# Linear attention on one NeuronCore: reciprocals spread and applied behind the fourth tile's V product, denominators ahead of the values product

## What is computed

```
x = x + attention(layernorm(x))      # linear attention, 16 heads of 32
x = x + ffn(layernorm(x))            # top-2 mixture of 8 experts

attention:  q = elu(xn Wq + bq) + 1, k = elu(xn Wk + bk) + 1, v = xn Wv + bv
            for each t:  kv += k_t v_t^T;  ksum += k_t
                         out_t = (q_t kv) / (q_t . ksum + 1e-6)
            result = out Wo + bo
```

## Time and profile before

| | us |
|---|---|
| median of 3 executions | 1915.71 (1914.94 to 1915.79) |
| the profiled execution, its own time | 1916.06 |
| its span in the profile | 1914.3 |
| TensorE busy | 1890.7 (99%) |
| VectorE busy | 1569.2 (82%) |
| GpSimd busy | 889.8 (46%) |
| ScalarE busy | 663.8 (35%) |
| granted TensorE clock | 0.998 of full speed |

### The profile page before, as it was taken

How to read it: one execution, slowest core, us unless ns; L and a number is a source line. 1 busy time by engine, 2 the same in 40 slices (tenths; PEclk the granted TensorE clock), 3 DMA queues, 4 the chain that set the end, 5 groups by cost and what they waited for, 6 DMA issues and landing times.

```text
span 1914.3 us, 60181 instructions
## 1 busy us (share of the span) xinstructions
PE 1890.7 (99%) x25412; PEld 1659.6 (87%) x25412; DVE 1569.2 (82%) x3356; ACT 663.8 (35%) x1298; POOL 889.8 (46%) x981
## 2 busy tenths in 40 slices
PE   7999999999999999999999999999999999999997
PEld 6888888888888888888888888888888888888887
DVE  7888787888879888778878888887888897888888
ACT  4333333323333332333333433333333333323331
POOL 4345554455443554534554445544345553455422
PEclk9999999999999999999999999999999999999999
DMA  6343234333243432343323334333443234333222
GB/s 215 101 128 112 96 106 128 118 118 112 90 127 119 127 121 74 123 125 116 123 89 118 117 112 136 100 98 113 128 128 112 85 114 130 117 117 113 89 73 90
DMA packets 171197, 217.97 MB, mean 114 GB/s; under 512 B 24368, under 2 KB 85808, under 8 KB 170928
## 3 DMA queue, kind: packets, MB, share of 16 engines
q1 hardware_dynamic: 170928, 214.13, 35.4%
HBM read 151.02 MB, written 63.04 MB: 112 GB/s over the span
## 4 chain that ended last, share of the span: by engine, by line
PE 95%; DVE 2%; POOL 1%; DMA 1%; issue 0%; SPq 0%; ACT 0%; POOLq 0%; DVEq 0%
PE ring L684 38%; PE ring L666 36%; PE ring L758 7%; PE num_ps L788 6%; PE num_ps L771 3%; PE num_ps L801 2%; PE ring L730 1%; PE ring L743 1%; DMA v_tok<-in_wv_t 1%; DVE s_mask L973 0%; PE ring L654 0%; DVE stats L1091 0%; DVE den L1220 0%; DVE res L1084 0%; DVE o_lo L1215 0%
## 5 line engine op out<-in xcount | busy, mean ns | idle before, releaser
L1315 POOL TENSOR_TENSOR k_sum<-k_sum,q_raw 128x512 f32<-128x512 f32 x128 | 165.3, 1291 | 545.0 <-DVE q_raw L984 545.0
L883 ACT ACTIVATE e_tmp<-ring,bias_n 128x512 f32<-128x512 f32 x256 | 175.9, 687 | 509.3 <-PE ring L666 508.7
L973 DVE TENSOR_TENSOR s_mask<-ring,causal 128x512 f32<-128x512 f32 x512 | 315.0, 677 | 0.0
L684 PE MATMUL ring<-wv_hi,xt_hi 128*128 128x260 f32 x1024 | 298.9, 292 | 0.0
L684 PE MATMUL ring<-wv_hi,xt_lo 128*128 128x260 f32 x1024 | 289.2, 282 | 0.0
L684 PE MATMUL ring<-wv_lo,xt_hi 128*128 128x260 f32 x1024 | 289.2, 282 | 0.0
L684 PE MATMUL ring<-wo_hi,o_hi 128*128 128x260 f32 x1016 | 284.8, 281 | 1.3 <-ACT o_hi L938 1.3
L684 PE MATMUL ring<-wo_lo,o_hi 128*128 128x260 f32 x1016 | 285.7, 282 | 0.0
L684 PE MATMUL ring<-wo_hi,o_lo 128*128 128x260 f32 x1016 | 285.5, 284 | 0.2 <-DVE o_lo L1215 0.2
L938 ACT ACTIVATE o_hi<-num_ps 128x512 fp32r<-128x512 f32 x127 | 75.8, 597 | 465.9 <-PE num_ps L788 465.9
L666 PE MATMUL ring<-xt_hi,wk_hi 128*128 128x512 f32 x512 | 207.2, 405 | 3.4 <-DVE xt_lo L1042 1.7
(11 more groups left out here) (147 smaller groups left out, 3955.4 us busy)
## 6 DMA issues: line engine op xcount, KB each, us to landing
x_tok<-in_x SPq DMA_DIRECT2D x128, 256.0 KB, 3.8
res<-in_x SPq DMA_DIRECT2D x128, 256.0 KB, 2.8
out<-res SPq DMA_DIRECT2D x128, 256.0 KB, 2.1
x_in<-in_x_t SPq DMA_DIRECT2D x124, 256.0 KB, 4.7
keys_turned<-k_turned SPq DMA_DIRECT2D x112, 256.0 KB, 2.0
k_tok<-keys_turned SPq DMA_DIRECT2D x448, 64.0 KB, 2.1
x_rows<-moments_rows SPq DMA_DIRECT2D x31, 512.0 KB, 3.6
k_t<-in_wk_t SPq DMA_DIRECT2D x4, 256.0 KB, 4.5
```

Source lines behind the costliest of these rows:

```text
L684: mm = pe.matmul(bank[:, 0:HW], rows[a](k), w[b][:, k, h, :], start=n == 0, stop=n == 3 * KD - 1)
L883: act.activation(e_tmp[:, m], bank, ACT.Relu, bias=bias_n[:, m, g:g + 1], scale=-1.0).then_inc(phi_relu.handle, 1)
L973: dve.tensor_tensor(s_mask[:, j], ring[:, st.bank(u)].rearrange("p (g t) -> p g t", g=KD), repeat(causal, KD), ALU.mult).then_inc(free[st. ...
L1315: pool.tensor_tensor(k_sum[:, g], k_sum[:, g], q_raw[:, g], ALU.mult).then_inc(prod.handle, 1)
```

## The change

- TensorE: in steps with attention, `spread_reciprocals` moves from behind O2 to behind V2, in front of `from_state` of tile 3. `denominators` moves from behind `from_tile` of tile 2 to between `add_state` and `from_tile`. The scores of tile 0 wait for R0 and R1 to be freed, and for a new semaphore `divided` (the first tile's columns of groups 2 and 3); the scores of tile 1 wait for R2 and R3 to be freed.
- ScalarE: the copy of the denominators goes ahead of that of `o_hi`.
- VectorE: `divide` is done behind V2's halves and no more ahead of the moments. It is cut in six: groups 0 and 1 whole, the first 128 columns of groups 2 and 3, then the other 384 columns of groups 2 and 3.
- The ring: R0 to R3 stand behind V2 in the list, and the three skipped uses all stand at the end of the step. So the banks of most uses change; K0's bank (0) was that of V3's first half and is that of its second.

```
-SKIPS = {0: 1, 3: 2}
+SKIPS = {3: 3}
...
         uses += chunk_uses(c, 0, 1)
+        uses += [("R", g) for g in range(KD)] * (c == 3)
         uses += [("DEN", 0)] * (c == 2) + scores_of((c + 1) % TPB) + chunk_uses(c, 2, 3)
-        uses += [("O", (c, 0)), ("O", (c, 1))] + [("R", g) for g in range(KD)] * (c == 2)
+        uses += [("O", (c, 0)), ("O", (c, 1))] 
...
             for u in scores_of(c):
                 pe.wait_ge(free[st.bank(u)].handle, st.claimed(u))
+            if c == 0:
+                for g in (0, 1):
+                    pe.wait_ge(free[BANK[("R", g)]].handle, st.freed(("R", g)))
+                pe.wait_ge(divided.handle, 2 * (off + 1))
+            if c == 1:
+                for g in (2, 3):
+                    pe.wait_ge(free[BANK[("R", g)]].handle, st.prev.freed(("R", g)))
             for g in range(KD):
-                if c == 0:
-                    pe.wait_ge(free[BANK[("R", g)]].handle, st.freed(("R", g)))
...
                     chunks(st, c, 0, 1)
+                if last and proj and attn:
+                    spread_reciprocals(st)
                 if attn:
...
                     from_state(st, c)
                     add_state(st, c)
+                    if c == 2 and proj:
+                        denominators(st)
                     from_tile(st, c)
...
                 if c == 2 and not attn:
                     sum_columns(pe)
-                if c == 2 and proj:
                     denominators(st)
...
-                if c == 2 and attn and proj:
-                    spread_reciprocals(st)
...
-        def divide(st):
-
-            for g in range(KD):
+        def divide(st, gs, t):
+
+            for g in gs:
                 u = ("R", g)
                 dve.wait_ge(full[st.bank(u)].handle, st.filled(u))
-                bank = ring[:, st.bank(u)]
-                dve.tensor_tensor(q_div[:, (st.off + 1) % 2, g], bank, q_raw[:, g], ALU.mult).then_inc(free[st.bank(u)].handle, 1)
+                ins = dve.tensor_tensor(q_div[:, (st.off + 1) % 2, g, t], ring[:, st.bank(u), t], q_raw[:, g, t], ALU.mult)
+                if t.stop < BT:
+                    ins.then_inc(divided.handle, 1)
+                else:
+                    ins.then_inc(free[st.bank(u)].handle, 1)
...
-                if last and proj and attn:
-                    divide(st)
                 if last and attn and proj:
                     residual_moments(st, 2)
                 if proj:
                     chunks(st, c, 0, 1)
-                if last and not attn:
-                    divide(st)
+                if last and proj:
+                    divide(st, (0, 1), slice(0, BT))
+                    divide(st, (2, 3), slice(0, P))
+                    divide(st, (2, 3), slice(P, BT))
```

More of the change, by code:

```diff
@@ L443, in attention @@
     k_scan, k_carried, prod = sem("k_scan"), sem("k_carried"), sem("prod")
-    den_rec, rden_hi, rden_parts = sem("den_rec"), sem("rden_hi"), sem("rden_parts")
+    divided, den_rec, rden_hi, rden_parts = sem("divided"), sem("den_rec"), sem("rden_hi"), sem("rden_parts")
     summed, lower_summed = sem("summed"), sem("lower_summed")
@@ L930, in body @@
                     exponential(act, 4)
+                if c == 2 and proj:
+                    u = ("DEN", 0)
+                    act.wait_ge(full[st.bank(u)].handle, st.filled(u))
+                    for m in part_begun(st.off - 1):
+                        act.wait_ge(chosen.handle, (m + 1) * CHOOSE_STEPS)
+                    act.activation(den, ring[:, st.bank(u), 0:BT // 2], ACT.Copy,
+                                   bias=DEN_EPS).then_inc(free[st.bank(u)].handle, 1)
                 if st.alone() and last:
@@ L938, in body @@
                     act.activation(o_wide[0], num, ACT.Copy).then_inc(o_hi.handle, 1)
[L939 to L945, removed]
                 if attn:
```

## The result

The changed kernel takes 1946.73 us (median of 4, 1946.32 to 1948.97) against 1915.75 for the kernel before: a ratio of 1.0164, 95% interval 1.0147 to 1.0182, 31 us slower. The forecast was 1940 and slower, with a range of 1928 to 1950.

The account below looks back on a forecast made before the run. The prediction took TensorE's own stream as the bound, with VectorE's late last xt_lo delaying K0: 24.3 us over steps 0 to 29, plus 0.5 at the first step, less 0.3 in step 30, gave +24.5, 1940 us; range 1928 to 1950.

Parts of the forecast that it names:

- The bound and the mechanism: TensorE's stream bounds; VectorE's later last xt_lo makes K0 wait, +0.76 us in even steps, +0.86 in odd; chance 0.76.
- the sum: 15 x 0.76 + 15 x 0.86 = 24.3 us for steps 0 to 29; with the first step and step 30, +24.5.
- TensorE's wake-up: At K0, TensorE starts 0.14 us after the VectorE operation it waits for.
- part 2: Denominators ahead of the values product: taken as 0 for TensorE, bounds -0.1 to +0.1 us a step.
- The start: First step adds 0.13 us for the division's pieces and 0.40 for K0's new bank: 0.5.
- Part 1: Spread reciprocals moved behind V2: saves TensorE 0.30 us a step, 9.3 over 31 steps, if TensorE can use it.
- the first rival: Gain without a wait at K0: 1906 us, or 1909 with 0.21 saved a step by the skill's rule; chance 0.07.
- part 3: VectorE divides behind V2's halves in six pieces, 2.53 us instead of 2.40, ending the last xt_lo at 940.03, not 938.74.
- VectorE idle for about 1.0 before V2's second half in each step: Sign of a right forecast: VectorE waits over 1 us for V2's second half, behind moments and V2's first half.
- The second mechanism: Tile 3's masks, 0.88 us later, free O2's bank too late; 1949 us at 0.3 a step; chance 0.12.
- The estimate from the Trainium skill: Two added division instructions on VectorE cost 0.31 us, 0.18 more a step than taken; 1945 us instead of 1940.
- The wait at the scores: At tile 0's scores TensorE waits 0 to 0.25 us, somewhat more in odd steps, vanishing in K0's larger wait.

Follow-up runs that it names:

- delay2: The kernel before with one more 128x512 addition on VectorE, output unused, in front of tile 3's first xt_lo: 1922.88 us, ratio 1.003.
- lo_on_gpsimd: The changed kernel with the first two xt_lo pieces in steps with attention computed by GpSimd, not VectorE: 1919.93 us, ratio 1.0016.
- den_back: The changed kernel with denominators behind the values product again and ScalarE's copy of them behind o_hi: 1945.6 us, ratio 1.0145.
- best_try: `lo_on_gpsimd` with the denominators' move undone as well, and step -1 dividing groups 2 and 3 ahead of 0 and 1: 1917.06 us, ratio 0.9999.
- late_wait: `best_try` with tile 0's scores waiting for `divided` only before group 2, and GpSimd's two xt_lo pieces in step -1 too: 1912.02 us, ratio 0.9985.
- fill_gap: `den_back` with the first two xt_lo pieces moved ahead of V2's halves on VectorE: 2008.71 us, ratio 1.0483.

## Why the prediction was right, and where it was not

**The bound and the mechanism: right.** TensorE was the bound, and the change made it wait at K0 for the last xt_lo, 30 times. `delay2` and `lo_on_gpsimd` show this from both sides. From one K0 to the next a step grew by 0.91 on average (K0 of step 30 lies 31.33 later than before, the second projection of step 0 already 4.02; (31.33 - 4.02)/30), against 0.81 in the sum. Three things make the difference. TensorE's wake-up was shorter than I took (956.92 to 956.98 is 0.06, not 0.14). A TensorE that has waited starts slowly: its second matmul follows after 0.34 instead of 0.23 (939.41 to 939.64 in the kernel before), a term of 0.11 that was missing. These two leave 0.03, and with part 2 undone a step grew by 0.84, just that. The other 0.07 a step, 2.2 us in all, comes with part 2, which the sum had at nothing.

**The start: mis-sized.** From the spread of step -1 to K0 of step 0 were 58.09 - 52.12 = 5.97 before and are 62.12 - 53.91 = 8.21 now: 2.2 instead of 0.5. I had seen K0's new bank, and overlooked V3's: in step -1 V3 comes right behind the spread and claims the banks of R2 and R3, so TensorE waits 2.2 us for the division. The profiled execution lost another 1.8 ahead of that spread (53.91 against 52.12): TensorE's granted clock was at 1.2 GHz, half of full speed, for 3.4 us from 34.3 on. That is not the change's: `delay2`, whose step -1 is that of the kernel before, has the same stretch and its spread at 54.26, and `den_back`, with the changed step -1, has no such stretch ahead of its spread and has it at 51.87. `best_try` halves the wait at V3 (1.1), as expected of it.

**Sum, of the two profiled executions.** Steps 0 to 29 cost 27.3 (forecast 24.3), the start 2.2 (0.5), the clock at the start 1.8 (not in the sum), and from K0 of step 30 to the end 0.9 was gained (0.3): 27.3 + 2.2 + 1.8 - 0.9 = 30.4, the difference of the spans. The forecast of 24.5 was 6 us short and its range held the result; where the 0.6 more at the end come from stays open.

**Part 1: the saving was mis-sized.** From V2's last full matmul to the state product are 947.18 - 946.53 = 0.65. In the kernel before, with no spread between them, they are 0.21:

```profile
930.34 0.28 PE L684 MATMUL ring<-wv_hi,xt_lo 128*128 128x260 f32 x1
930.55 0.67 PE L771 MATMUL num_ps<-q_div,kv_diag 64*32 64x128 f32 x32
```

So the spread adds 0.44 in its new place and had added 0.53 + 0.10 in the old one. It saves 0.19, not 0.30; `late_wait`, where TensorE has no such wait left, shows 0.17 a step. The figure in the first rival that goes with the Trainium skill, "TensorEngine Tiling (Array Packing)", section "Key Properties" (0.21, a change from one small tile to another drains too), was nearer than my own.

**Part 2: wrong, and hidden.** "Taken as 0" failed as a price: alone it costs 23 us. I had shifted VectorE's tile 2 by 0.88 and kept every length, as if it had no neighbour. That the total came out right was luck in this: the idle gap of part 3, which I did see, was there to be eaten, and so part 2 cost 2.2 us and not 23. The forecast "VectorE idle for about 1.0 before V2's second half in each step" was wrong for most steps of the changed kernel, and right for `den_back`. The second mechanism that I had named, O2 waiting for late masks, did not occur: no such wait is in the changed kernel's list.

**Part 3: right.** Six pieces took 2.52 (947.34 to 949.86), 2.53 in the sum. The estimate from the Trainium skill, "VectorE: DVE Perf Modes" (0.18 a step more), is not borne out. I had quoted its section "The DRAIN you can't avoid" in part: it also says that a next operation that is not held starts earlier, which is what the pieces do.

**The wait at the scores**: 16 waits, 4.7 us in all, and swallowed by the one at K0, as forecast.

## What to carry to other kernels

When the bound engine has a helper with half a microsecond of cover, list that helper's last deliveries and their slack before moving anything: a saving of 0.19 us on TensorE was bought here with 1.3 us of delay on VectorE (940.03 - 938.74 in the sum). Price a shift on VectorE with GpSimd's timeline beside it, since here an operation with two SBUF inputs that landed early in a long GpSimd operation lasted until its end. And test parts alone: their costs can hide in each other's gaps, so the sum of the parts (23 + 28 = 51 us here, against 29 to 31) says little about the whole.

## What was not expected of the hardware

- A 128x256 operation of VectorE on two SBUF tensors took 0.47 to 1.89 us by where in a GpSimd operation of 1.6 us it started; in `fill_gap` a pair of 128x512 ones took 3.54 instead of 1.28 us, and TensorE, which waited up to 2.9 us for what came behind them, fell to 1.2 GHz for 3.4 or 6.8 us 13 times.
- After a wait, TensorE's first full matmul shows 0.50 and the second starts 0.34 behind it, against 0.39 and 0.23 (939.41 to 939.64 in the trace of before).
- A change from one small tile shape to another is not free on TensorE: between V2 and the state product the spread adds 0.44, of which 0.21 are its streams by the prediction's estimate, so the added boundary costs some 0.23.
